# Choosing the tokens of four experts: all thresholds from one product, slots split by bitwise instructions

## What is computed

```python
logits = flat_x @ Wg + bg
top_vals, top_idx = jax.lax.top_k(logits, 2)
probs = softmax(sparse logits of the two)
for i in range(4):
    assigned = (top_idx == i).any(axis=-1)
    score = where(assigned, probs[:, i], -inf)
    sel_p, sel_idx = jax.lax.top_k(score, 512)
    tok = flat_x[sel_idx]
    y = gelu(tok @ W1[i]) @ W2[i] * p          # 512x2048, 2048x512
    out = out.at[sel_idx].add(y)
```

## Time and profile before

| | us |
|---|---|
| runs | 620.23, 622.01, 619.1 (median 620.23) |
| profiled execution | 620.21 |
| its span | 618.4 |
| TensorE busy in the span | 580.6 |
| VectorE busy | 354.2 |
| ScalarE busy | 281.2 |
| GpSimd busy | 187.3 |

### The profile page before, as it was taken

The page is one execution under the profiler, slowest core; times in us unless marked ns, Lnnn a source line. Parts: engine busy times, 40 slices in busy tenths (PEclk is TensorE's granted clock), DMA queues, the critical chain, the costliest instruction groups (busy, mean ns, idle before and its releaser), DMA issues.

```text
span 618.4 us, 8885 instructions
## 1 busy us (share of the span) xinstructions
PE 580.6 (94%) x2921; PEld 409.9 (66%) x2924; DVE 354.2 (57%) x701; ACT 281.2 (45%) x421; POOL 187.3 (30%) x142
## 2 busy tenths in 40 slices
PE   8999999999998636999999999999999999999994
PEld 3445555554554413788888888888888788888883
DVE  6889898998988783543344633444534355423212
ACT  3877767767777220532433434324324324333220
POOL 8465566566552216000310420400510401500002
PEclk9999999999999957999999999999999999999997
DMA  4623323423213115223323452333451532542001
GB/s 147 205 69 121 120 88 118 136 87 119 86 53 103 68 68 187 86 74 131 117 87 134 141 188 80 119 112 109 157 183 68 157 113 81 172 157 68 1 0 68
DMA packets 46600, 67.73 MB, mean 110 GB/s; under 512 B 8560, under 2 KB 25072, under 8 KB 46576
## 3 DMA queue, kind: packets, MB, share of 16 engines
q1 hardware_dynamic: 42736, 54.84, 26.8%
q0 software_dynamic: 3840, 12.59, 6.0%
HBM read 54.70 MB, written 12.64 MB: 109 GB/s over the span
## 4 chain that ended last, share of the span: by engine, by line
PE 69%; DVE 5%; issue 1%; DMA 1%; ACT 1%; POOL 0%; POOLq 0%; DVEq 0%
PE two L1456 29%; PE four L1486 9%; PE four L1485 9%; PE four L1483 9%; PE two L1292 3%; PE four L1282 2%; PE two L1304 1%; DMA x_got<-x2n_dram,idx_all 1%; DVE junk L1059 1%; PE bank_t L1320 1%; PE bank_m L1444 1%; PE four L1327 1%; PE bank_t L1444 1%; PE bank_t L1312 1%; DVE onehot L1146 0%
## 5 line engine op out<-in xcount | busy, mean ns | idle before, releaser
L772 ACT ACTIVATE h_f<-two 128x512 f32<-128x512 f32 x64 | 38.3, 599 | 229.2 <-PE two L1456 229.2
L1222 DVE TENSOR_TENSOR h_lo<-h_f,h_hi 128x512 fp32r<-128x512 f32 x64 | 44.1, 690 | 123.7 <-ACT h_hi L773 123.7
L1456 PE MATMUL two<-xt_hi,w_hi 128*128 (+1 forms) x256 | 101.9, 398 | 0.7 <-ACT xt_hi L761 0.7
L1486 PE MATMUL four<-w_hi,h_lo 128*128 128x512 f32 x256 | 100.5, 393 | 0.0
L1483 PE MATMUL four<-w_hi,h_hi 128*128 128x512 f32 x256 | 100.5, 392 | 0.0
L1485 PE MATMUL four<-w_lo,h_hi 128*128 128x512 f32 x256 | 100.4, 392 | 0.0
L1456 PE MATMUL two<-xt_hi,w_lo 128*128 (+1 forms) x256 | 100.3, 392 | 0.0
L1456 PE MATMUL two<-xt_lo,w_hi 128*128 (+1 forms) x256 | 100.1, 393 | 0.0
L666 ACT ACTIVATE prob<-four,rnorm 128x512 f32<-128x512 f32 x128 | 77.6, 690 | 28.4 <-POOL rnorm L478 19.0
L1190 DVE TENSOR_TENSOR w_lo<-raw,w_hi 128x2048 fp32r<-128x2048 f32 x31 | 71.0, 2290 | 23.3 <-ACT w_hi L699 23.3
L478 POOL TENSOR_TENSOR rnorm<-ss_max,power 128x8 f32<-128x8 f32 x32 | 64.7, 2025 | 49.7 <-DVE ss_max L821 43.8
(11 more groups left out here) (182 smaller groups left out, 758.3 us busy)
## 6 DMA issues: line engine op xcount, KB each, us to landing
raw<-in_L_ffn_W SPq DMA_DIRECT2D x64, 512.0 KB, 4.5
x_all<-in_x SPq DMA_DIRECT2D x16, 256.0 KB, 2.8
c_sb<-in_ctx SPq DMA_DIRECT2D x16, 256.0 KB, 2.9
out<-x_all SPq DMA_DIRECT2D x16, 256.0 KB, 2.0
x2n_dram<-x2n SPq DMA_DIRECT2D x16, 256.0 KB, 2.0
p_inv<-inv_dram SPq DMA_DIRECT2D x30, 128.0 KB, 2.9
few<-p_sum SPq DMA_DIRECT2D x30, 2.0 KB, 2.2
cst<-in_consts SPq DMA_DIRECT2D x1, 354.5 KB, 5.0
```

The source lines that it names most:

```text
L772: nc.scalar.activation(h_f[m % 2][:, :], z_ps[m % 2][:, :], ACT.Gelu)
L1222: nc.vector.tensor_tensor(h_lo[m % 2][:, :], h_f[m % 2][:, :], h_hi[m % 2][:, :].bitcast(F32), ALU.subtract).then_inc(h_split, 1)
L1456: return nc.tensor.matmul(z[:, :], w_part[c][:, w], x_k, start=start, stop=stop)
L1486: last = nc.tensor.matmul(acc_ps[:, t, :], h_lo[m % 2][:, h], w_hi[c][:, w], start=False, stop=(m == MT - 1))
```

## The change

Three things. The round before the last also spreads its new `low` over four columns (`lowpick`), and the product with ones brings it to all partitions during the last count. The last `enough` is spread over four columns by its owner mask `C_OWN` (which expert a partition belongs to), and the last round's product is with ones in place of `block_b`, so that its result is the number of all four experts on all partitions; the two ends `t_low` and `t_high` come straight from it. Slots are carried with 2^23 added (`WHOLE`), where the bits of an f32 number are its integer; a bitwise "and" with one pattern leaves the low seven bits (`s_lo`), with another the rest (`s_hi`), and the tables that they are compared with have 2^23 added. The constants grow by 138 columns.

```diff
-C_ALL = C_RESET + E * 2 * UNITS
+C_OWN = C_RESET + E * 2 * UNITS
+C_COUNT = C_OWN + E
+C_PLACE = C_COUNT + P
+C_LOWBITS = C_PLACE + ST
+C_HIGHBITS = C_LOWBITS + 1
+C_ALL = C_HIGHBITS + 1
+WHOLE = 2.0 ** 23
...
+    c[:, C_OWN:C_COUNT] = p[:, None] // WAYS == np.arange(E)[None, :]
+    c[:, C_COUNT:C_PLACE] = WHOLE + p[None, :]
+    c[:, C_PLACE:C_LOWBITS] = WHOLE + P * np.arange(ST)[None, :]
+    c[:, C_LOWBITS] = WHOLE + P - 1
+    c[:, C_HIGHBITS] = WHOLE + 2 * NO_SLOT - P
...
-                nc.vector.scalar_tensor_tensor(enough[:, :], count[:, :], 2.0, (excess if r else rest0)[:, :],
-                                               ALU.mult, ALU.is_ge).then_inc(enough_done, 1)
+                if final:
+                    link(nc.vector.scalar_tensor_tensor(enough_f[:, :], count[:, :], 2.0, excess[:, :],
+                                                        ALU.mult, ALU.is_ge))
+                    nc.vector.tensor_scalar(enough_e[:, :], cst[:, C_OWN:C_OWN + E], enough_f[:, 0:1], None, ALU.mult
+                                            ).then_inc(enough_done, 1)
+                    dve.wait_ge(t_ready, 1)
+                    put(nc.vector.tensor_copy(low_e[:, :], bank_t[:, 0:E]))
+                    put(nc.vector.tensor_scalar(next_e[:, :], bank_t[:, 0:E], width, None, ALU.add))
+                else:
+                    nc.vector.scalar_tensor_tensor(enough[:, :], count[:, :], 2.0, (excess if r else rest0)[:, :],
+                                                   ALU.mult, ALU.is_ge).then_inc(enough_done, 1)
...
-                    put(nc.vector.tensor_scalar(n_next[:, :], n_enough, 1.0, None, ALU.add))
-                    link(nc.vector.scalar_tensor_tensor(low_new[:, :], n_enough, width, low[:, :],
-                                                        ALU.mult, ALU.add))
-                    link(nc.vector.scalar_tensor_tensor(high[:, :], n_next[:, :], width, low[:, :],
+                    put(nc.vector.scalar_tensor_tensor(t_low[:, :], bank_m[:, 0:E], width, low_e[:, :],
+                                                       ALU.mult, ALU.add))
+                    link(nc.vector.scalar_tensor_tensor(t_high[:, :], bank_m[:, 0:E], width, next_e[:, :],
                                                         ALU.mult, ALU.add))
...
-            for n, end_of in enumerate((low_new, high)):
-                nc.vector.tensor_scalar(lowpick[:, n, :], cst[:, C_PICK:C_PICK + E], end_of[:, 0:1], None, ALU.mult
-                                        ).then_inc(pick_done, 1)
-            dve.wait_ge(t_ready, 1)
-            put(nc.vector.tensor_copy(t_low[:, :], bank_t[:, 0:E]))
-            link(nc.vector.tensor_copy(t_high[:, :], bank_t[:, E:2 * E]))
+                    nc.vector.tensor_scalar(lowpick[:, :], cst[:, C_PICK:C_PICK + E], low[:, 0:1], None, ALU.mult
+                                            ).then_inc(pick_done, 1)
...
-            put(nc.vector.tensor_scalar(s_c[:, :, :], ge[:, :, :], -NO_SLOT, NO_SLOT, ALU.mult, ALU.add))
+            put(nc.vector.tensor_scalar(s_c[:, :, :], ge[:, :, :], -NO_SLOT, NO_SLOT + WHOLE, ALU.mult, ALU.add))
...
-            link(nc.vector.tensor_scalar(s_hi[:, :, :], slot[:, :, :], float(P), None, ALU.is_ge))
-            for s in range(2, ST):
-                link(nc.vector.scalar_tensor_tensor(s_hi[:, :, :], slot[:, :, :], float(s * P), s_hi[:, :, :],
-                                                    ALU.is_ge, ALU.add))
-            link(nc.vector.scalar_tensor_tensor(s_lo[:, :, :], s_hi[:, :, :], -float(P), slot[:, :, :],
-                                                ALU.mult, ALU.add))
+            def bits(col):
+                return cst[:, col:col + 1].unsqueeze(2).broadcast_to([P, E, UNITS]).bitcast(U32)
+            put(nc.vector.tensor_tensor(s_lo[:, :, :].bitcast(U32), slot[:, :, :].bitcast(U32), bits(C_LOWBITS),
+                                        ALU.bitwise_and))
+            link(nc.vector.tensor_tensor(s_hi[:, :, :].bitcast(U32), slot[:, :, :].bitcast(U32), bits(C_HIGHBITS),
+                                         ALU.bitwise_and))
...
             for r in range(ROUNDS):
-                pe.wait_ge(enough_done, r + 1)
-                nc.tensor.matmul(bank_m[:, 0:1], block_b[:, :], enough[:, :], start=True, stop=True
-                                 ).then_inc(n_ready, 1)
-            pe.wait_ge(pick_done, 2)
-            nc.tensor.matmul(bank_t[:, 0:2 * E], cst[:, C_ONES:C_ONES + P],
-                             lowpick[:, :, :].rearrange("p n e -> p (n e)"), start=True, stop=True
-                             ).then_inc(t_ready, 1)
+                if r == ROUNDS - 1:
+                    pe.wait_ge(pick_done, 1)
+                    nc.tensor.matmul(bank_t[:, 0:E], cst[:, C_ONES:C_ONES + P], lowpick[:, :], start=True, stop=True
+                                     ).then_inc(t_ready, 1)
+                    pe.wait_ge(enough_done, r + 1)
+                    nc.tensor.matmul(bank_m[:, 0:E], ones_b[:, :], enough_e[:, :], start=True, stop=True
+                                     ).then_inc(n_ready, 1)
+                else:
+                    pe.wait_ge(enough_done, r + 1)
+                    nc.tensor.matmul(bank_m[:, 0:1], block_b[:, :], enough[:, :], start=True, stop=True
+                                     ).then_inc(n_ready, 1)
```

More of the change, by code:

```diff
@@ L89, in constants @@
     c[:, C_SELF:C_SELF + E * E] = (j == i) * -1e30
-    c[:, C_RESET:C_ALL] = np.arange(E * 2 * UNITS) % (2 * UNITS) != 0
+    c[:, C_RESET:C_OWN] = np.arange(E * 2 * UNITS) % (2 * UNITS) != 0
+    c[:, C_OWN:C_COUNT] = p[:, None] // WAYS == np.arange(E)[None, :]
[3 more added lines that the diff above has]
+    c[:, C_HIGHBITS] = WHOLE + 2 * NO_SLOT - P
     return c
@@ L137, in xattn_moe_kernel @@
         rest0 = keep("rest0", [P, 1])
[L138 to L141, removed]
+        lowpick = keep("lowpick", [P, E])
+        enough_f = keep("enough_f", [P, 1])
+        enough_e = keep("enough_e", [P, E], BF16)
+        low_e = keep("low_e", [P, E])
+        next_e = keep("next_e", [P, E])
         t_low = keep("t_low", [P, E])
@@ L1146, in one_hot @@
                 nc.vector.tensor_tensor(onehot[:, a:b, :],
-                                        cst[:, C_IOTA:C_IOTA + P].unsqueeze(1).broadcast_to(shape),
+                                        cst[:, C_COUNT:C_COUNT + P].unsqueeze(1).broadcast_to(shape),
                                         s_lo[:, bass.ds(e, 1), a:b].rearrange("p a t -> p (a t)").unsqueeze(2)
@@ L1154, in payload @@
                 link(nc.vector.tensor_tensor(sel[:, e, :, :], s_hi[:, e, :].unsqueeze(2).broadcast_to(shape),
-                                             cst[:, C_IOTA:C_IOTA + ST].unsqueeze(1).broadcast_to(shape),
+                                             cst[:, C_PLACE:C_PLACE + ST].unsqueeze(1).broadcast_to(shape),
                                              ALU.is_equal))
```

## The result

The changed kernel takes 616.35 us (median of 6, 615.31 to 617.56), before 620.03 (median of 6 in the same comparison). The ratio is 0.9934 with a 95% interval of 0.9915 to 0.9954: 4.1 us less by the ratio, 2.9 to 5.3. The forecast was 618.5 with a low end of 616.8. The profiled execution took 617.56 with a span of 615.8; it is 2.65 shorter than the profiled execution of before (620.21).

A forecast was written before the change was run, and what follows sets the result against it. The serial stretch between attention and experts, paced by the spacing of VectorE's small linked instructions, was taken as the bound. Thresholds net 1.17 + slots 0.57 = 1.74; 620.2 − 1.7 = 618.5 us, range 616.8 to 620.6.

The forecast's parts named there:

- Thresholds: From the last comparison to the first use of the thresholds: 1.04 us in place of 2.29, 1.25 us gone.
- lowpick ahead of the count: One more VectorE instruction between the new thr and the last count, costed in full at 0.08 us, bounds 0.07 and 0.22.
- the pair low_e, next_e: Two new instructions between the spread and the wait for its product, costed at nothing; uncovered, at most 0.3 us together.
- Slots: Two bitwise instructions replace four linked ones: 0.44 us in place of 1.01, 0.57 gained; bounds 0.71 gained to 0.07 lost.
- Idle products: TensorE's idle products ahead of find: margin before find's start sinks from 0.98 to 0.41 us, costed at nothing.
- rival 3: Slots hidden by idle products or loads beside the gather, only thresholds count: 619.0 us; chance 0.18 together with rival 4.
- rival 4: Thresholds not shortened, the pair and four-column operations late by 0.5 us together: 619.0 us; chance 0.18 together with rival 3.
- The step that failed: Expert phase: TensorE full from the first expert product on, the phase's length unchanged, so gains ahead of it count at the end.
- a loss, of 0.4: Load of constants, 138 columns longer: costed at nothing, with 0.4 us as bound for a late row of an early unit.
- my sum's assumption: Between routing and first expert products: the clock levels, 1.2 and 2.4 GHz, move with the work; otherwise 617.3 or 621.2 us.
- rival 1: The clock adds: all transposes of the first tokens at 2.4 GHz, 1.2 us more gained, 617.3 us; chance 0.16.
- rival 2: The clock takes: 1.2 GHz over first expert products and transposes costs 2.7 us against 1.74 gained, 621.2 us; chance 0.08.

The follow-up runs named there:

- e6: The whole change against the kernel before, all its tiles at their old addresses and the load of constants of the same size: 618.09 us, ratio 0.9970.

## Why the prediction was wrong

- *Thresholds:* 1.04 us, as forecast. lowpick ahead of the count: the count starts 0.26 behind thr (222.94 to 223.20) where it was 0.25 before (222.50 to 222.75): 0.01 in place of 0.08. Right, and the pair low_e, next_e stayed hidden.
- *Slots:* 0.39 in place of 0.44. Right; the upper bound of 0.54 for a bitwise instruction was far too wide.
- *Idle products:* they ran at 1.2 GHz until 230.55, into the first quarter of find, which starts 0.91 behind the first one-hot (229.43 to 230.34) where it was 0.83 before. The last quarter decides, and it starts 2.55 behind the first one-hot in both (229.43 to 231.98, 230.85 to 233.40). Nothing of the 0.62 was lost; rival 3 falls, and rival 4 with the first point.
- *The step that failed* is the one that closes the sum: "TensorE full from the first expert product on, with that phase's length unchanged". TensorE was full, but the phase is 1.2 us shorter in the traces, and moving the tiles alone (e1) gave 2.0 (0.9 to 3.1) in the times. The sum had no term for where tiles lie; the new small tiles it did not cost at all, and the 138 columns as a transfer alone. As a transfer they were harmless, as argued (423.5 KB landed 5.2 after its issue, the first user ran at 13.65). In the table above they are harmless in place as well, since their 544 bytes moved weights and activations alike. What took the difference d from 32 to 64 modulo 256 are the 32 bytes by which the small tiles grew; no run has the columns or the small tiles alone, so this split rests on the table. For this part of the edit the forecast's bounds held only a loss, of 0.4, so its low end of 616.8 was too high. What of e1's 2.0 lies beyond the 1.2 is inside its interval and was not located.
- *The clock.* The two levels did not move with the work. The twelve products that spread most of the keys come 1.1 us sooner in the changed kernel, behind the same 0.41 of idleness. Before, the granted clock was 1.00 under them; now it falls to 0.50. The lines of before, then those of the changed kernel:

```profile
200.92 1.50 PE L1393 MATMUL four<-cst,key_w 128*128 128x128 f32 x12 [0.41 <-ACT key_w L740]
201.00:202.00 1.00, 1.00 (x10) 1.00 (x11) 0.92 (x5) 0.00 (x0) 0.27 (x1) 1.00 0.60 238
```

```profile
199.83 2.06 PE L1411 MATMUL four<-cst,key_w 128*128 128x128 f32 x12 [0.41 <-ACT key_w L752]
200.00:201.00 1.00, 1.00 (x9) 1.00 (x9) 0.53 (x2) 0.00 (x0) 0.42 (x1) 0.81 0.00 0
201.00:202.00 1.00, 1.00 (x6) 0.77 (x5) 0.92 (x5) 0.00 (x0) 0.36 (x1) 0.50 0.67 256
```

  This agrees with the Trainium skill, "TensorE: Matmul & The Clock Gate", section "Part 1: The HAM clock gate (the "warmup" mystery)", that the window does not start with the kernel; my sum's assumption was wrong there. It cost time, at a place that the prediction had not looked at, ahead of the search. From the first copy of the keys to the last, before and changed:

```profile
199.31 1.47 ACT L740 ACTIVATE key_w<-key 128x1536 f32<-128x1536 f32 x1
210.45 0.43 DVE L1044 COPY key_w<-key 128x512 f32<-128x512 f32 x1
```

```profile
198.21 1.47 ACT L752 ACTIVATE key_w<-key 128x1536 f32<-128x1536 f32 x1
210.88 0.43 DVE L1056 COPY key_w<-key 128x512 f32<-128x512 f32 x1
```

  These are 11.14 us before and 12.67 after, 1.5 more. The stretch begins 1.1 sooner, which makes up for most of it; 0.43 remains, and that is the 0.44 by which the comparison comes later. Over all nineteen profiles the stretch takes 12.66 to 13.27 us in the eight where the clock is at 1.2 GHz in a part of it, and 11.14 to 12.09 in the other eleven; both groups have kernels with and without the change. Behind the search the clock took nothing on balance: transposes to first product took 5.61 in place of 5.89, at a mean clock of 0.69 and 0.71, so neither rival 1 nor rival 2 came, and the gather took 7.87 in place of 7.58. From the gather's issue to the first expert product the nineteen profiles have 11.8 to 14.0 us. Such differences are likely a part of the 3 us by which executions of one kernel differ; with one profile for each kernel that is not shown.

The sum of what was forecast was right to 0.13 us (1.87 for 1.74 from the comparison on), and the change at unmoved addresses (e6) gave 1.9 (0.7 to 3.0). What was missing was a term for the layout, 1.2 us by the traces. The 4.1 by the times is more than the 2.65 between the two profiles: the profiled execution is the slowest of the changed kernel's six, and in it the 1.5 of the clock went against the change.

## What to carry to other kernels

An edit that adds or resizes an on-chip tile moves every tile behind it: compare the spacing of unchanged products before and after, and where a change is tried by halves, hold all addresses fixed and check that no load was added. In this kernel the weights that TensorE reads belong at the same remainder of 256 bytes as the activations. Whether some buffers are slow can be read from the chain's repeated groups, buffer by buffer. One unused tile of 192 bytes took 3.9 us off the expert phase, more than the 1.9 of the change.

## What the runs showed of the hardware

- Back-to-back products of 512 columns in f32 (`float32r`) start 0.2267 us apart when weights and activations have the same remainder of 256 bytes. Otherwise a block of 24 takes up to 5.61 in place of 5.44, that is up to 0.2338 for each, by the remainder (32, 64, 96 and 128 were tried). With the engine full and the clock at 1.00 in both, neither view by shares shows it.
- Bitwise "and" of 128x64 32-bit patterns, one operand a broadcast column: 0.22 to 0.23 us, start to start 0.14 where independent.
- One further load of 69 KB at the start cost 1.4 us (0.2 to 2.6); a wait for a small DMA some 60 us later is 0.5 longer in its profile, and how the two hang together was not found.
- The same twelve products behind the same idle time met a granted clock of 1.00 in one execution and of 0.81 and 0.50 in another, and the stretch around them took 1.5 us more.
